# Attention scores: the four full-precision products of a half unit ahead of its twelve split products

## What is computed

```python
q = (hidden_states @ Wq.T).reshape(b, s, H, D).transpose(0, 2, 1, 3)      # s = 256, H = 32, D = 128
...
scores = jnp.einsum('bhqd,bhkd->bhqk', q, k) * scale
causal = jnp.tril(jnp.ones((s, s), dtype=bool))
scores = jnp.where(causal, scores, jnp.asarray(-1000000000.0, scores.dtype))
attn = jax.nn.softmax(scores, axis=-1)
out = jnp.einsum('bhqk,bhkd->bhqd', attn, v)
out = out.transpose(0, 2, 1, 3).reshape(b, s, H * D)
return out @ Wo.T
```

## Time and profile before

| | |
|---|---|
| median of three runs | 1680.99 us |
| the profiled execution | 1679.91 us |
| its span, first to last instruction | 1678.0 us |
| attention, from 288 us to 1296 us of the span | 1008 us |
| two units (first pair and second pair) | 64.8 us |

### The profile page before, as it was taken

One profiled execution on the slowest core, in us unless ns is written; L12 is line 12 of the kernel. 1 busy time (PEld: TensorE's weight loads), 2 busy tenths in 40 slices (PEclk: granted clock), 3 DMA queues, 4 the chain that ended last, 5 costly groups with the idle time before them and its releaser, 6 DMA issues. The chain is left out here.

```text
span 1678.0 us, 26468 instructions
## 1 busy us (share of the span) xinstructions
PE 1631.0 (97%) x8298; PEld 1370.3 (82%) x8298; DVE 1164.2 (69%) x2990; ACT 924.4 (55%) x2464; POOL 843.8 (50%) x1257
## 2 busy tenths in 40 slices
PE   6989999999999999999999999999999899999999
PEld 4868887788888888888888888888888788877887
DVE  6883254776776776667667767767767588787776
ACT  3764455665765665666566556657657443434432
POOL 4883003634634644544445346446446297708752
PEclk9999999999999999999999999999999999999999
DMA  5011754111111111134111111111110021113111
GB/s 170 26 29 60 274 178 145 51 63 38 51 64 38 41 51 54 46 101 163 64 40 50 63 39 51 63 39 51 64 38 26 32 76 63 39 32 113 51 51 50
DMA packets 62489, 114.98 MB, mean 69 GB/s; under 512 B 5584, under 2 KB 25040, under 8 KB 58256
## 3 DMA queue, kind: packets, MB, share of 16 engines
q1 hardware_dynamic: 62352, 113.30, 20.4%
HBM read 84.97 MB, written 28.31 MB: 68 GB/s over the span
## 5 line engine op out<-in xcount | busy, mean ns | idle before, releaser
L1854 PE MATMUL ps_q<-kv_w_hi,o_hi 128*128 128x512 f32 x512 | 203.5, 397 | 4.5 <-DVE o_lo L72 4.5
L1854 PE MATMUL ps_q<-kv_w_lo,o_hi 128*128 128x512 f32 x512 | 200.0, 391 | 0.0
L1854 PE MATMUL ps_q<-kv_w_hi,o_lo 128*128 128x512 f32 x512 | 199.7, 390 | 0.0
L72 POOL TENSOR_TENSOR kv_w_lo<-w_raw,kv_w_hi 128x512 fp32r<-128x512 f32 x128 | 163.1, 1291 | 57.3 <-ACT kv_w_hi L67 57.3
L1796 PE MATMUL ps_q<-h_hi,kv_w_hi 128*128 128x512 f32 x448 | 181.9, 406 | 3.0 <-PEq L1092 1.5
L1796 PE MATMUL ps_q<-h_lo,kv_w_hi 128*128 128x512 f32 x448 | 175.4, 392 | 0.0
L1796 PE MATMUL ps_q<-h_hi,kv_w_lo 128*128 128x512 f32 x448 | 175.0, 391 | 0.0
L67 ACT ACTIVATE kv_w_hi<-w_raw 128x512 fp32r<-128x512 f32 (+1 forms) x240 | 126.6, 566 | 64.1 <-POOL w_raw L260 62.8
L1383 POOL TENSOR_SCALAR prob<-prob,inv_sum 128x128 f32<-128x128 f32 x256 | 95.3, 372 | 103.6 <-DVE inv_sum L1601 103.3
L67 ACT ACTIVATE o_hi<-ps_o 128x512 fp32r<-128x512 f32 x128 | 76.3, 596 | 127.2 <-PE ps_o L1836 127.1
L1439 ACT ACTIVATE prob<-prob,neg_max 128x128 f32<-128x128 f32 x256 | 100.2, 392 | 83.0 <-DVE neg_max L1596 83.0
(11 more groups left out here) (236 smaller groups left out, 4868.1 us busy)
## 6 DMA issues: line engine op xcount, KB each, us to landing
w_raw<-in_wq_g SPq DMA_DIRECT2D x16, 1024.0 KB, 4.8
w_raw<-in_wo_g SPq DMA_DIRECT2D x16, 1024.0 KB, 4.7
k_raw<-k_scratch SPq DMA_DIRECT2D x32, 256.0 KB, 3.4
v_raw<-v_scratch SPq DMA_DIRECT2D x32, 256.0 KB, 3.8
f_gate_raw<-in_gate_c SPq DMA_DIRECT2D x10, 512.0 KB, 4.9
f_up_raw<-in_up_c SPq DMA_DIRECT2D x10, 512.0 KB, 3.6
f_down_raw<-in_down_c SPq DMA_DIRECT2D x10, 512.0 KB, 4.0
x<-in_x SPq DMA_DIRECT2D x16, 256.0 KB, 2.8
```

The lines of the kernel that those rows point to most:

```text
L72: return dve.tensor_tensor(parts[LO], src, parts[HI].bitcast(F32), ALU.subtract)
L1854: done = pe.matmul(ps_q[:, half, :], o[b][i][:, half, h, :], wo[j][:, h, :], start=(h == 0 and m == 0), stop=(h == GROUP - 1 and m == 2))
```

## The change

In `scores` the loop over the heads is split in two. The first loop does the waits and the full-precision product of each of the four heads, the second the three split matmuls of each head and the increment of `s_done`. All 20 matmuls, their operands and the waits stay; no other engine's program changes.

```diff
@@ -1808,6 +1808,7 @@
                             else:
                                 pe.wait_ge(t_lo, 6 * u)
                         pe.matmul(ps_s[:, h, 0:P], q_first[:, h, b, :], k_raw[:, b, 0:P], start=True, stop=True)
+                    for h in range(GROUP):
                         for m, (i, j) in enumerate(PASSES):
                             done = pe.matmul(ps_s[:, h, 2 * P:4 * P], q_second[i][:, h, b, :], k[j][:, b, :], start=(m == 0), stop=(m == 2))
                         done.then_inc(s_done, 1)
```

## The result

The changed kernel takes 1701.28 us (median; 1700.24 to 1702.21), the kernel before 1681.01. The ratio is 1.0122, with an interval of 1.0104 to 1.0140: the change costs 20 us. Forecast were 1701.3.

What follows compares the result with a forecast made beforehand. PE's stream, busy 97% of the span, was taken as the bound. Second pairs 11.3, first pairs 8.8 and the last pair 0.15 sum to 20.3 us on 1679.91, 1700.2; the runs' median adds 1.08: 1701.3 us, range 1693 to 1706.

Steps and rivals of the forecast that it cites:

- PE's own stream: PE's 20 score matmuls in each half: 0.03 us less, to 2.28 to 2.29; bounds -0.10 and +0.10.
- The first head's signal: First head's s_done in each half: 0.65 us later, behind six more full-precision matmuls of 0.109 each.
- the smaller term: Skill's rule of about 81 ns a matmul: first signal 0.49 us later, sum at the end about 13 us.
- Second pair, b = 0: PE's wait for DVE's add to x has no slack: 0.62 us more in each of 15 units.
- Second pair, the third flip: Second pair, b = 1: later prob_lo delays the third flip by 0.13 us, between 0 and 0.25.
- First pair, b = 1: P3 of block 1 starts 0.55 us later through ACT's prob_hi and DVE's prob_lo and U4; bounds 0.35 and 0.65.
- Unit 0: Unit 0's first pair has the same 0.55 us as the other 15, making 16 x 0.55 = 8.8 us.
- What was covered: PE's wait behind output(u, 1, 0) moves along, weight load keeps 0.9 us of cover, new scored waits are met.
- Rival (a): Only the existing wait for the add grows, ACT and DVE chain has slack: 9.3 us, 1690.3; 11%.
- (b): Rival: faster, fewer turns between matmul kinds and DVE's delay absorbed; 1679.1, at the bound 1674.6 us; 3%.
- (d): Rival: no difference, both kinds take PE the same time and waits are met; 1681 within 3.4 us; 5%.
- (c): Rival: both delays at upper bounds (0.87, 0.65), runs of eight cost PE 0.10 a half; 30 us, 1711; 5%.

Runs made afterwards that it cites:

- e1_second_b0: Kernel before, with the new order only in half 0 of the 15 second pairs; +11.4 us, ratio 1.0065.
- e9_after_add_act: e7_after_add_first, with ACT's prob_hi ahead of head 2's exponentials and DVE's prob_lo and U4 ahead of its inverse in the first pair; 1680.25 us.
- e2_first_b1: Kernel before, with the new order only in half 1 of the 16 first pairs; +8.3 us, ratio 1.0050.
- e3_other_halves: Kernel before, with the new order only in half 0 of first pairs and half 1 of second pairs (and of the last); +3.2 us, ratio 1.0019.
- e7_after_add_first: Changed kernel, with DVE's add of the second pair ahead of the four scores of half 0 instead of behind them; 1686.87 us.

## Why the prediction was right

- **PE's own stream: the sign was wrong, at a small size.** Expected -0.03 a half, measured +0.01 (2.315 to 2.324). The steps that failed are the two prices of a matmul in a long run: eight full-precision ones take (1.05 - 0.275) / 7 = 0.111 each and not the transposes' 0.109, 0.01 in all, and the split ones 0.120 and not 0.117, 0.03 in all. The half of 2.28 us that the prediction gave as a sign of being right was 2.32. The bounds held it.
- **The first head's signal.** 0.65 us expected, 1.58 - 0.91 = 0.67 measured, by the same 0.111; the 0.49 us of the smaller term that the prediction weighs beside it is out. DVE's four heads took 2.23 (2.24 expected).
- **Second pair, b = 0.** 0.62 expected, 0.627 measured (e1_second_b0, with the order in these halves alone: 0.627).
- **Second pair, the third flip.** 0.13 expected, 0.087 measured: `prob_lo` and U2 follow one another as in the sum, and the load's 0.11 is not exposed in full: the flip's first transpose starts 0.02 later, and the step to its second is 0.165 and not 0.110.
- **First pair, b = 1.** 0.55 expected, 0.587 in the changed kernel, 0.573 with the order in that half alone; with the 0.027 of half 0 the whole first pair is 0.61 longer. The chain's steps came nearly as worked out: counted from the pair's start, as the prediction does, `prob_hi` +0.61 and U4 of block 1 +0.59, where both were forecast at +0.62. P3 of block 0 was late by 0.13 (0.92 after the flips and not 0.79) where 0.06 had been forecast, but it is hidden in the delay that follows; only e9_after_add_act, which takes that away, lays it bare.
- **The repeats** took 19.5 us more; the two pairs' terms, (0.75 + 0.55) x 15, were 19.5. Two units take 66.14 us by the stretches; 66.1 were forecast.
- **Unit 0: the size was right, the step wrong.** The prediction gave it the first pair's 0.55 by half 1. e2_first_b1, with the new order in that half, has unit 0 only 0.03 longer; e3_other_halves, with the new order in half 0 of unit 0, has it 0.7 longer, and so has e7_after_add_first. There DVE's scores of half 1 stand behind half 0's `inverse`, which are late with half 0's scores, and PE's wait for these scores ahead of the flips grows from 0.24 to 0.91 us.
- **What was covered stayed covered.** The wait behind `output(u, 1, 0)` is the same 4.5 us, and PE's list has no line for the load of the weights or for the added waits for `scored` ahead of the scores. The load's cover was thinner than the 0.9 us worked out in two of the 15 repeats: ACT waits 0.4 us for it in each.
- **Rival (a)** had 11% and would have been the first pair without a loss. e2_first_b1 says +8.3 for it alone. **(b)** and **(d)** are out by the result, **(c)** by the half of 2.32 us and by delays that stayed below its 0.87 and 0.65.

That the total agrees to a tenth is partly luck. In the profiled execution the stretch ahead of unit 0, which the change doesn't touch, is 2.7 us shorter, unit 0 is 1.8 longer, unit 31 is 0.25 longer (0.15 forecast for it), and what follows the attention is 1.4 longer. (The attention's last output product starts at 1319.0 in the kernel before; the 1296 of the table above is where the last unit's flips have begun.) The clock moves with the first, the second and the last of these. Ahead of unit 0 it is 0.98 on average before and 0.99 after. Behind the attention PE waits 2.06 us for a split (`h_lo`) in both kernels; in the changed one the clock falls to 0.50 1.5 us after the wait, and the 22 matmuls behind the wait take 5.1 us and not 3.9. In unit 0 it falls too, after a wait of 2.15 us by the row, and its scores start at the lower of the two levels, 1.2 GHz:

```profile
285.27 2.05 PE L1810 MATMUL ps_s<-k_raw,q_first 128*128 128x128 f32 x8 [2.15 <-DVE kv_w_lo L72]
```

The row of unit 0 (its start rounded up to 285.30) has the granted clock as its third number from the end:

```profile
285.30:317.44 32.14, 30.61 (x154) 25.35 (x155) 22.49 (x67) 20.07 (x60) 18.07 (x25) 0.95 0.24 83
```

Eight full-precision matmuls take 2.05 us here and 1.05 elsewhere, and the granted clock of unit 0 is 0.95 on average where the same unit of the kernel before has 1.00. The wait ahead was as long in the kernel before, and there the clock stood at the upper level. What the lower level costs unit 0 as a whole is less than it costs the scores: e1_second_b0 has the old order in unit 0 and the same 0.95, and takes 31.09 us for it, 0.75 more than the kernel before; its half 0 is 1.56 longer and its half 1 0.81 shorter. With the order's 0.7 this makes 1.4 to 1.5 of the 1.8; the rest stays open.

## What to carry to other kernels

Regrouping work on an engine that is full can cost nothing on that engine, as here, and still moves the moment at which the first result is signalled; ask first how much later the first one comes, then follow it through each queue to the next wait of the full engine, and see whether that wait already stands in the list. A wait there with no slack passes the delay on in full. A wait that isn't in the list may be met by 0.15 us only, and that is read from the order of time alone. Before reordering the full engine, look at what stands ahead of the awaited instruction on the other one: two such moves on DVE gave 15 us.

## What the runs showed of the hardware

Turning from one kind of matmul to the other cost PE nothing that the rows show, where I had half expected a price. Full-precision matmuls of 128 columns step by 0.108 to 0.114 us and split ones of 256 columns by 0.117 to 0.120, in runs of two, three, eight or twelve; with 2 turns between the kinds in a half or with 8, the 20 of them take 2.32 us. I had not expected that the step isn't constant: in the old order it varies from head to head (0.108 to 0.114 for a full-precision matmul behind another), in a long run of one kind it settles at 0.111 to 0.112 and at 0.120, and so the new order won nothing. Why, these runs don't show.

The granted clock is not the same in every execution of one program (0.993 to 0.998 for the kernel before). After the same wait of PE, 2.15 us ahead of unit 0's scores and 2.06 us behind the attention, it fell to 1.2 GHz in the profiled execution of the changed kernel and stayed at 2.4 in that of the kernel before. The stretches outside the repeats move with it, and so the prices here are read from the repeats.
